# Attention and feed-forward block: the value products as three rows of eight 256-column matmuls

## What is computed

```python
def reference(x, Wqkv, Wout, w1, w2, w3):        # x: 1 x 2048 x 256, 16 heads of 128
    xn = layernorm(x)
    q, k, v = split(einsum('bsd,ed->bse', xn, Wqkv))
    logits = einsum('bqhd,bkhd->bhqk', q, k) * 128 ** -0.5
    w = softmax(logits)
    attn = einsum('bhqk,bkhd->bqhd', w, v).reshape(B, S, H * D)
    hidden = sigmoid(xn @ quantize(w1).T) * (xn @ quantize(w2).T)
    return x + einsum('bse,de->bsd', attn, Wout) + hidden @ quantize(w3).T
```

## Time and profile before

| | |
|---|---|
| median of 3 runs | 1920.66 us (1920.07 to 1921.25) |
| profiled execution | 1918.09 us |
| its span, first to last instruction | 1916.3 us |
| granted TensorE clock, mean | 0.996 |
| PE busy | 1873.7 us, 9540 matmuls |
| DVE busy | 1648.0 us |
| POOL busy | 1352.1 us |
| ACT busy | 1253.9 us |

### The profile page before, as it was taken

The page is one execution under the profiler, slowest core; times in us unless marked ns, Lnnn a source line. Parts: engine busy times, 40 slices in busy tenths (PEclk is TensorE's granted clock), DMA queues, the critical chain, the costliest instruction groups (busy, mean ns, idle before and its releaser), DMA issues.

```text
span 1916.3 us, 29455 instructions
## 1 busy us (share of the span) xinstructions
PE 1873.7 (98%) x9540; PEld 1583.2 (83%) x9540; DVE 1648.0 (86%) x2216; ACT 1253.9 (65%) x1700; POOL 1352.1 (71%) x514
## 2 busy tenths in 40 slices
PE   5979999999999999999999999999999999999998
PEld 4868888888888888888888888888888888888887
DVE  6368898898989889898989989898998989889895
ACT  3437676766767676666767666676766667666664
POOL 2418687776868777686877768687776868777685
PEclk9999999999999999999999999999999999999999
DMA  3037677676767767676776767677676767767664
GB/s 106 0 81 174 156 171 171 156 170 158 173 156 173 172 151 172 158 170 157 174 170 152 171 158 170 158 173 171 152 170 158 169 159 170 174 147 168 156 159 128
DMA packets 195827, 298.59 MB, mean 156 GB/s; under 512 B 37888, under 2 KB 57024, under 8 KB 195776
## 3 DMA queue, kind: packets, MB, share of 16 engines
q1 hardware_dynamic: 195776, 298.01, 66.5%
HBM read 12.65 MB, written 2.10 MB: 8 GB/s over the span
## 4 chain that ended last, share of the span: by engine, by line
PE 90%; DVE 3%; SPq 2%; POOL 2%; ACT 1%; issue 1%; DMA 1%; DVEq 0%; POOLq 0%; ACTq 0%
PE ps_o L375 23%; PE ps_o L377 12%; PE ps_s L367 11%; PE ps_s L369 11%; PE ps_s L368 11%; PE ps_s L338 5%; PE ps_t L357 4%; PE ps_t L347 4%; SPq L284 2%; PE ps_s L410 2%; PE ps_o L385 1%; PE ps_o L387 1%; PE ps_o L386 1%; POOL parts L1044 1%; DVE prob L896 1%
## 5 line engine op out<-in xcount | busy, mean ns | idle before, releaser
L1044 POOL TENSOR_TENSOR parts<-raw,parts 128x2048 fp32r<-128x2048 f32 x254 | 1176.8, 4634 | 446.0 <-ACT parts L674 445.1
L686 ACT ACTIVATE prob<-ps_s,neg_max 128x1024 f32<-128x1024 f32 x512 | 567.4, 1115 | 470.9 <-DVE neg_max L890 470.9
L375 PE MATMUL ps_o<-parts,v_hi 128*128 128x512 f32 x2032 | 728.7, 397 | 2.6 <-POOL v_lo L1037 2.6
L886 DVE TENSOR_REDUCE row_max<-ps_s 128x1 f32<-128x1024 f32 x512 | 612.2, 1213 | 68.8 <-PE ps_s L369 49.5
L896 DVE STREAM_TRANSPOSE prob<-prob 128x1024 f32<-128x1024 f32 x508 | 599.5, 1218 | 57.6 <-ACT prob L686 57.2
L377 PE MATMUL ps_o<-parts,v_lo 128*128 128x256 f32 x2032 | 571.2, 281 | 0.0
L674 ACT CAST parts<-raw 128x2048 fp32r<-128x2048 f32 x254 | 486.7, 1916 | 87.9 <-DMA raw<-prob 86.7
L375 PEld LDWEIGHTS ps_o<-parts,v_hi 128*128 128x128 f32 x2032 | 382.3, 188 | 91.3 <-issue 3.9
L367 PE MATMUL ps_s<-k_hi,q_hi 128*128 128x512 f32 x1024 | 404.7, 395 | 11.6 <-ACT prob L686 11.0
L369 PE MATMUL ps_s<-k_hi,q_lo 128*128 128x512 f32 x1024 | 400.8, 391 | 0.0
L368 PE MATMUL ps_s<-k_lo,q_hi 128*128 128x512 f32 x1024 | 400.3, 391 | 0.0
(11 more groups left out here) (113 smaller groups left out, 1630.2 us busy)
## 6 DMA issues: line engine op xcount, KB each, us to landing
raw<-prob SPq DMA_DIRECT2D x2032, 128.0 KB, 2.4
v_raw<-v_turned SPq DMA_DIRECT2D x244, 64.0 KB, 2.0
w_raw<-wqkv_dram SPq DMA_DIRECT2D x32, 128.0 KB, 2.5
y<-x_dram SPq DMA_DIRECT2D x4, 512.0 KB, 6.0
wo_raw<-wqkv_dram SPq DMA_DIRECT2D x16, 128.0 KB, 2.5
wo_raw<-wo_dram SPq DMA_DIRECT2D x16, 128.0 KB, 2.3
out_dram<-y SPq DMA_DIRECT2D x8, 256.0 KB, 2.7
w_raw<-w_dram SPq DMA_DIRECT2D x2, 704.0 KB, 10.6
```

The source lines that it names most:

```text
L375: nc.tensor.matmul(ps_pv, v_hi[:, kb, :], parts[:, kb].rearrange("p s a q -> p (s a q)"), start=(kb == 0), stop=False, skip_group_check=True)
L686: nc.scalar.activation(tile, logit, ACT.Exp, bias=neg_max[:, t:t + 1], scale=SCALE, accum_out=row_sum[:, t, half:half + 1]).then_inc(s_exp, 1)
L886: nc.vector.reduce_max(row_max[:, t, half:half + 1], ps_s[:, 2 * half:2 * half + 2, :].rearrange("p b n -> p (b n)"), AX_X).then_inc(s_mx, 1)
L1044: nc.gpsimd.tensor_tensor(half_of(0, half), moved(p, half), half_of(1, half), ALU.subtract).then_inc(s_pl, 1)
```

## The change

`products` and `products_last` no longer have 512-column matmuls. For half of the keys there are three rows of eight matmuls, each of 256 columns and all into the same 256 columns of PSUM: `v_hi` by the high parts, `v_hi` by the low parts, `v_lo` by the high parts. The sum of the three is then complete in PSUM, and the low part of the output is a single subtraction; the second DVE step, its semaphore and its wait go.

```diff
-        ps_pv = ps_o[:, 0, :]
-        ps_pv_lo = ps_o[:, 0, 0:2 * P]
-        ps_pv_hi = ps_o[:, 0, 2 * P:4 * P]
+        ps_pv = ps_o[:, 0, 0:2 * P]
...
-        ps_last = ps_v[0]
+        ps_last = ps_t[:, 0, 0:2 * P]
...
             def products(half):
-                for kb in range(half * KH, half * KH + KH):
-                    nc.tensor.matmul(ps_pv, v_hi[:, kb, :], parts[:, kb].rearrange("p s a q -> p (s a q)"),
-                                     start=(kb == 0), stop=False, skip_group_check=True)
-                    last = nc.tensor.matmul(ps_pv_hi, v_lo[:, kb, :], parts[:, kb, 1].rearrange("p a q -> p (a q)"),
-                                            start=False, stop=(kb == T - 1), skip_group_check=True)
+                for v, which in ((v_hi, 1), (v_hi, 0), (v_lo, 1)):
+                    for kb in range(half * KH, half * KH + KH):
+                        last = nc.tensor.matmul(ps_pv, v[:, kb, :], parts[:, kb, which].rearrange("p a q -> p (a q)"),
+                                                start=(kb == 0 and v is v_hi and which == 1),
+                                                stop=(kb == T - 1 and v is v_lo))
                 last.then_inc(s_pv, 1)
...
             def products_last(half):
-                for b in range(KH):
-                    kb = half * KH + b
-                    nc.tensor.matmul(ps_last, v_hi[:, kb, :], last_parts[half][:, b].rearrange("p s q -> p (s q)"),
-                                     start=(kb == 0), stop=False, skip_group_check=True)
-                    last = nc.tensor.matmul(ps_last[:, 2 * P:4 * P], v_lo[:, kb, :], last_parts[half][:, b, 1],
-                                            start=False, stop=(kb == T - 1), skip_group_check=True)
+                for v, which in ((v_hi, 1), (v_hi, 0), (v_lo, 1)):
+                    for b in range(KH):
+                        kb = half * KH + b
+                        last = nc.tensor.matmul(ps_last, v[:, kb, :], last_parts[half][:, b, which],
+                                                start=(kb == 0 and v is v_hi and which == 1),
+                                                stop=(kb == T - 1 and v is v_lo))
                 last.then_inc(s_lpv, 1)
...
             def output_low(h, p):
                 dve.wait_ge(s_ohi, count(8, h, p + 1))
-                nc.vector.tensor_tensor(o_lo[:], ps_pv_hi, o_hi[:], ALU.subtract).then_inc(s_orest, 1)
-                dve.wait_ge(s_orest, count(8, h, p + 1))
-                nc.vector.tensor_tensor(o_lo[:], ps_pv_lo, o_lo[:].bitcast(F32), ALU.add).then_inc(s_olo, 1)
+                nc.vector.tensor_tensor(o_lo[:], ps_pv, o_hi[:], ALU.subtract).then_inc(s_olo, 1)
```

More of the change, by code:

```diff
@@ L229, in build @@
         s_ohi = sem("output_high_ready")
-        s_orest = sem("output_rest_ready")
         s_olo = sem("output_low_ready")
@@ L661, in output_high @@
                     act.wait_ge(s_y, count(8, h, p))
-                nc.scalar.copy(o_hi[:], ps_pv_hi).then_inc(s_ohi, 1)
+                nc.scalar.copy(o_hi[:], ps_pv).then_inc(s_ohi, 1)
             def last_high(n):
@@ L756, in _ @@
             act.wait_ge(s_y, count(8, end, 7))
-            nc.scalar.copy(o_hi[:], ps_last[:, 2 * P:4 * P]).then_inc(s_ohi, 1)
+            nc.scalar.copy(o_hi[:], ps_last).then_inc(s_ohi, 1)
         @block.vector
@@ L996, in _ @@
             dve.wait_ge(s_ohi, count(8, end, 8))
-            nc.vector.tensor_tensor(o_lo[:], ps_last[:, 2 * P:4 * P], o_hi[:], ALU.subtract).then_inc(s_orest, 1)
-            dve.wait_ge(s_orest, count(8, end, 8))
-            nc.vector.tensor_tensor(o_lo[:], ps_last[:, 0:2 * P], o_lo[:].bitcast(F32), ALU.add).then_inc(s_olo, 1)
+            nc.vector.tensor_tensor(o_lo[:], ps_last, o_hi[:], ALU.subtract).then_inc(s_olo, 1)
             result(end, 7)
```

## The result

The changed kernel takes 1910.57 us, the median of 5 runs (1908.24 to 1911.48), against 1920.07 us for the kernel before (5 runs, 1917.29 to 1921.25). The ratio is 0.9953, with a 95% interval from 0.994 to 0.9966: 0.47% faster. The forecast was 1929.4 us, 0.46% slower, with a range from 1917.5 to 1938.5; the sign was wrong, and that 0.46 and 0.47 look alike is chance. The profiled execution took 1910.57 us, its span 1908.7 (before 1918.09 and 1916.3), so 7.6 us of span went.

What follows compares the result with a forecast made beforehand. TensorE, busy 98%, was taken as the bound; +9.2 us of matmul spacing less 0.45 at the end gave +8.8, so 1926.9 us profiled and, with 2.57 to the median, 1929.4 us (0.46% slower), range 1917.5 to 1938.5.

Steps and rivals of the forecast that it cites:

- What bounds the kernel: Whole run: TensorE busy 98% of the span, 111.55 of 111.60 us in a middle head, so its matmul spacing counts in full.
- The spacing of 256-column matmuls: In products: 2048 pairs of 0.3525 us become triples of 0.3570 us, +9.2 us.
- r: Start-to-start spacing of 256-column matmuls following each other without end in products; taken as 0.119 us, break-even 0.1175.
- rival 3: In products: 256-column steps run at 0.11, more exactly 0.1133 us; -25.6 us, 1894.6 us; chance 0.09 with its smaller form.
- The split into a share of columns and a fixed share: Cross-check from logits steps: 256 columns cost 0.1067 us, each matmul 0.0133 besides; pair 0.3467, triple 0.3600.
- rival 2: In products: price is per matmul and larger than elsewhere, triple 0.3688 us; +33.3 us, 1953.5 us; chance 0.06 with anything dearer.
- The 0.006 of a pair left unexplained: In products: a 512-and-256-column pair takes 0.3525 us, cross-check gives 0.3467; some 0.006 from alternation or operands, main uncertainty.
- The trail behind products: Seven 512-column steps after a half take 1.62 us against 1.59; between -7.7 and +7.7 us, taken as 0.
- DVE's step: Dropping output_low's second step, 53.9 us of DVE: 0 in the heads, -0.45 us at the kernel's end.
- Loads, order within the half, ACT: In products, extra weight loads overlap and new order moves no wait; ScalarE's copy and rounding unaffected: 0 each.
- rival 3's smaller form: The slower steps after products vanish, -7.7 us, with 256-column spacing 0.1175 us: 1912.5 us; within the shared chance 0.09.
- The rule cited from the Trainium skill: Warm matmuls start N / 2.4 + 2.5 ns apart: pair 325.0 ns, triple 327.5 ns, so +5.1 us in products.

Runs made afterwards that it cites:

- the split: The changed kernel with three of out_projection's six matmuls ahead of the first half of products and three ahead of the second: 1906.94 us, ratio 0.9938.
- two column ranges: The kernel before with only its 512-column matmuls split, v_hi by low into its own 256 columns, DVE keeping both steps: 1910.12 us, ratio 0.996.
- eight of 512 and eight of 256: The kernel before with the same 16 matmuls of a half reordered, eight of 512 columns then eight of 256, instead of alternating: 1910.72 us, ratio 0.9959.
- the split alone: The kernel before with out_projection split over the two tiles and nothing else changed: 1921.07 us (11 runs), ratio 1.0014.

## Why the prediction was wrong

**What bounds the kernel: right.** PE is full before and after, 110.95 of 111.00 us.

**The spacing of 256-column matmuls: this step failed.** The whole sum hung on r, taken as 0.119 (+9.2 us) with break-even at 0.1175. Measured is 0.11627 on average over the products, and 0.3529 a pair before (steps over 0.3 us left out): 2048 x (3 x 0.11627 - 0.3529) = -8.4 us where +9.2 stood. The rows were read rightly, and the choice between them was wrong in kind: I took r for a property of the matmul, to be read off the nearest row, and weighed 0.120 against 0.118. It is a state of the run, with at least three levels, and neither `out_projection` nor `ffn_down` stays at the quickest. The 0.11 of the earlier trace rows was in my hands; rival 3 named it, 0.1133, and got 0.09 because no run kept it up. In the changed kernel a good half of the runs do. Had they all, as nearly with the split, the spacing would have been worth 2048 x (0.353 - 3 x 0.1141) = 22 us; had none, nothing.

**The split into a share of columns and a fixed share: misled.** It made 0.120 look lawful (0.0133 a matmul, in 512 and 256 columns alike). 0.1133 is just half of the 0.2267 of logits: in the quick state a matmul of 256 columns pays no fixed share at all beyond what a 512-column one pays per column. The sentence that no 256-column step shows 0.123 isn't quite so: 11 of some 3000 in the kernel before lie at 123 to 130 ns. It bore on rival 2 alone.

**The 0.006 of a pair left unexplained: the place to stop.** It was named the main uncertainty, and both cases built on it (it goes with the alternation, it belongs to the operands) missed: it wasn't a fixed extra of either kind. The 512-column step in products is 0.234 whether beside 256-column steps (0.235) or its like (0.234); why it isn't 0.2267 there is still open.

**The trail behind products: its size was right, its value wrongly taken as 0.** The mean spacing of logits went from 228.34 to 227.65 ns (3072 of them, -2.1 us) and that of keys, queries and values from 229.66 to 227.20 (1152, -2.8 us): -4.9 us, within the bound of -7.7. Position by position, the seven 512-column steps behind a half were 228 to 236 ns on average; now only the first three are above 227, at 229 to 230.

**A new wait: missing.** -8.4 and -4.9 make -13.3 us; the end gave 0.46, and the full clock of the last six matmuls another 0.42 (0.98 us where they took 1.40). The span lost 7.6. Some 6 to 7 us came back at starts that are later than their spacing. The 767 steps out of `out_projection` take 98.8 us where they took 95.4, mostly at a head's first pair, where PE waits for POOL's `v_lo` (2.6 us, now 4.8), and the steps over 0.3 us behind keys, queries and values grew by 2.1 us. With no step left out, the starts add up: products went from 725.3 to 717.5 us, logits from 717.7 to 715.4, keys, queries and values from 269.7 to 268.9, `out_projection` from 95.4 to 98.8, together -7.5. The earlier trace rows had the wait for `v_lo`, 2.6 us in three places, and the prediction passed over it; I had looked at whether a slower PE would absorb anything, not at what a quicker PE would run into.

**DVE's step: right.** Nothing in the heads (with the second step kept: 0.9958, without: 0.9953), 0.46 us at the end. **Loads, order within the half, ACT: right.** Key block by key block makes no difference.

**The range and the rule.** The range began at 1917.5 and rival 3's smaller form, r = 0.1175 with the trail gone, gave 1912.5 us: 1.9 us from the measured time, but by another sum, so the nearness is luck. The rule cited from the Trainium skill ("TensorE: Matmul & The Clock Gate", section "Back-to-back issue gap") would have given +5.1 us, the same wrong sign. The section gives that formula for an isolated matmul and says that in a stream of weight loads and matmuls the two together set the spacing; the prediction left this out. Its 109.2 ns for 256 columns is below all three spacings that the traces show (113.3, 118, 120), and a rule with one number per size has no place for them.

## What to carry to other kernels

Where TensorE is the bound, take the spacing between starts from the trace for each neighbourhood of a matmul, not for each shape: here the same 24 matmuls took 2.74 or 2.83 us, by how the run began. Trying the order of a few matmuls costs no work. Equal sizes together were worth 0.41% in the kernel before, as much as the change itself. Three small ones ahead of each long run took another 10 us of spacing from the changed kernel, of which 4.6 us of span were left (one profile each), and cost 0.14% in the kernel before, which has no such runs: an order is worth trying anew in each kernel. Where a step is moved to an engine with slack, read its duration there: 0.42 us expected was 3.95. And if the forecast turns on 1% of a spacing, the nearest row isn't near enough; say so with chances near one half.

## What the runs showed of the hardware

- In products, a run of 256-column matmuls, each with its own load of 128 columns, is at 118 ns, mostly from its first step, or falls to 113.3 after one to five steps, and stays there for the rest of its 24. Behind logits (512 columns at 227 ns) it settled at 118 in 105 of 110 halves, behind three or six matmuls of `out_projection` at 113.3 in nearly all (119 of 124 and 124 of 126), behind one of them mostly at 118. The kind or size of the neighbour isn't all: eight 256-column matmuls behind 512-column ones of products at 233 ns went to 113 in most halves, and behind `values` it was 113.3 in 14 of 15 halves that began late, while in the kernel with `out_projection` behind the first half, where they began in time, all 15 settled at 118. What counts seems to be how the first steps fall, which these runs don't take apart.
- In the recorded starts the three differ in the distance from a weight load to its matmul: 110 ns in the quick state, 114 to 115 in the middle one, 118 in the slow one, while the load mostly starts 2 to 5 ns after the matmul ahead in all three. A step of 121 to 125 ns stands ahead of the fall to 113 in 131 of 144 runs.
- `products_last`, with the same weights but other moving data and another bank, settled at 120 ns after eight steps in both its halves. What of it decides, the addresses, the bank or the start, wasn't tried. The runs of `ffn_down`, to changing banks, mostly don't settle: their steps go round between 115 and 122 ns. But in the first call, behind a stretch at the 1.2 GHz level, the steps held 120 ns 22 times over in the changed kernel and went round between 115 and 120 in the kernel before.
- The last six matmuls of the program ran at full clock (granted 1.00) after a stop of 1.37 us. In the kernel before they ran at 0.63 after a stop of 1.83 us, but the stop alone isn't the cause: four other kernels here stop for 1.83 us at that place, and their last six ran at 1.00. They are those with DVE's second step kept, with two column ranges, with eight of 512 and eight of 256, and with the split alone. The slower clock came in one profiled execution of the kernel before, and no run ties it to the change.
- A DVE subtraction of 256 columns with both inputs in SBUF took 3.8 to 4.3 us when it began during a POOL subtraction of 2048 columns, and 0.44 us in the one head where it began before it. One with an input in PSUM took 0.42 us beside the same POOL steps.

The six matmuls in the kernel with the second step kept, as windows:

```profile
1905.20:1906.25 1.05, 0.98 (x6) 0.78 (x6) 0.00 (x0) 0.00 (x0) 0.00 (x0) 1.00 0.73 250
```
